# Self-attention probabilities transposed by VectorE in 32x32 squares and rearranged by sixteen SBUF transfers, in place of TensorE transposes

## The reference, cut to what matters

```python
step = s // 4
scale = q[:, ::step].reshape(b, -1)
qk = jnp.einsum('bsd,btd->bst', q, k)
scaled_qk = qk * scale[:, None, :]
softmax_qk = jax.nn.softmax(scaled_qk, axis=-1)
return jnp.einsum('bst,btv->bsv', softmax_qk, v)
...
x = x + _L0_attn_ref(_layernorm(x, axis=-1), L0_attn_k, L0_attn_v, L0_attn_scale_factor, L0_attn_dropout_p)
```

## Time and profile before

| | |
|---|---|
| median of the three runs | 3894.85 us |
| lowest, highest | 3888.32, 3895.75 us |
| span of the profiled execution, first to last instruction | 3891.2 us |
| TensorE busy in that span | 3788.4 us (97%) |
| VectorE, ScalarE, GpSimd busy | 2395.0, 1432.7, 1534.5 us |
| the attention's tile loop | about 28 to 817 us of the span |

### The profile page before, as it was taken

One profiled execution on the slowest core, in us unless ns is written; L12 is line 12 of the kernel. 1 busy time (PEld: TensorE's weight loads), 2 busy tenths in 40 slices (PEclk: granted clock), 3 DMA queues, 4 the chain that ended last, 5 costly groups with the idle time before them and its releaser, 6 DMA issues. The chain is left out here.

```text
span 3891.2 us, 63669 instructions
## 1 busy us (share of the span) xinstructions
PE 3788.4 (97%) x19001; PEld 2532.2 (65%) x19161; DVE 2395.0 (62%) x6222; ACT 1432.7 (37%) x1793; POOL 1534.5 (39%) x860
## 2 busy tenths in 40 slices
PE   8999999999999899999999999999999999999998
PEld 7888888888877444544444444544444777777776
DVE  6544444444458688888888788878887533433135
ACT  3111222233224455455545555445555221222332
POOL 1000000000013667766677666766665222312234
PEclk9999999999999999999999999999999999999999
DMA  4001000145555322222112222222111433328579
GB/s 157 32 32 32 32 32 32 44 172 178 191 179 186 94 57 55 57 57 46 35 38 57 58 57 58 54 57 55 33 36 49 151 126 132 114 92 278 185 263 332
DMA packets 223177, 381.89 MB, mean 98 GB/s; under 512 B 17544, under 2 KB 102056, under 8 KB 222892
## 3 DMA queue, kind: packets, MB, share of 16 engines
q1 hardware_dynamic: 192876, 301.34, 26.7%
q0 software_dynamic: 14752, 49.29, 3.5%
q10 hardware_dynamic: 15264, 27.79, 1.9%
HBM read 229.71 MB, written 148.66 MB: 97 GB/s over the span
## 5 line engine op out<-in xcount | busy, mean ns | idle before, releaser
L1103 DVE CUSTOM_DVE_ANT_0 xf_unread<-xa_mx_ps,mask_q 128x402 bf16<-128x402 f32 x1984 | 1036.0, 573 | 290.3 <-PE xa_mx_ps L1096 156.7
L1726 ACT ACTIVATE probs<-xa_scores 128x1024 f32<-128x1024 f32 (+1 forms) x416 | 417.5, 1024 | 417.0 <-PE xa_scores L1600 371.6
L1726 ACT ACTIVATE xa_probs<-xa_scores 128x1024 f32<-128x1024 f32 (+1 forms) x416 | 417.3, 1024 | 397.8 <-PE xa_scores L1600 355.1
L1561 POOL TENSOR_TENSOR xa_sums<-xa_sums,xa_probs 128x1024 f32<-128x1024 f32 x220 | 519.7, 2383 | 18.1 <-POOL xa_sums L1561 15.7
L1561 POOL TENSOR_TENSOR xa_sums<-xa_sums,probs 128x1024 f32<-128x1024 f32 x220 | 519.3, 2381 | 18.9 <-POOL xa_sums L1561 15.3
L1600 PE MATMUL xa_scores<-mask_t,ident_b 128*128 128x512 bf16 (+1 forms) x1505 | 499.7, 387 | 5.3 <-issue 0.2
L1096 PE MATMUL xa_mx_ps<-xa_kp,queries 96*128 96x402 f32 x1024 | 364.2, 418 | 0.8
L1096 PE MATMUL xa_mx_ps<-xf_kp,queries 96*128 96x402 f32 x960 | 341.5, 418 | 0.4
L1594 PE MATMUL xa_scores<-queries,xf_kp 97*128 97x512 f32 (+1 forms) x832 | 284.2, 423 | 16.3 <-ACTq L1748 8.2
L1096 PEld LDWEIGHTS xa_mx_ps<-xa_kp,queries 96*128 96x128 f32 x1024 | 181.7, 189 | 172.2 <-DVE xf_maxima L1103 111.6
L1594 PE MATMUL xa_scores<-queries,xa_kp 97*128 97x512 f32 (+1 forms) x832 | 284.7, 423 | 1.8 <-ACT probs L1726 1.8
(11 more groups left out here) (415 smaller groups left out, 7388.0 us busy)
## 6 DMA issues: line engine op xcount, KB each, us to landing
bridge_rows<-sorted_in SPq DMA_DIRECT2D x78, 256.0 KB
sorted_out<-ex_made ACTq DMA_DIRECT2D x78, 256.0 KB
queries<-qT_high SPq DMA_DIRECT2D x30, 512.0 KB
xf_kp<-kT_high SPq DMA_DIRECT2D x16, 800.5 KB, 12.4
xa_kp<-kT_high SPq DMA_DIRECT2D x16, 800.5 KB
rows<-in_ctx SPq DMA_DIRECT2D x16, 768.0 KB, 5.1
values<-cxl_v SPq DMA_DIRECT2D x48, 256.0 KB
kT_high<-cxl_kT_high SPq DMA_DIRECT2D x12, 768.0 KB, 4.0
```

The costliest lines, as they stand in the source:

```text
L1103: return dve.tensor_tensor_reduce(out=unread[slot % 2][:, :], in0=scores[:, 0:MKEYS], in1=mask_q[:, half * QB + qt, MFIRST[kb]:MFIRST[kb] ...
L1561: pool.tensor_tensor(sums[pr][:, :, :], left[pr][:, :, :], right[pr][:, :, :], ALU.add).then_inc(pool_added, 1)
L1726: act.activation(prob[ring][pr][0:keys, :, :], scores[pr][0:keys, :, :], ACT.Exp, scale=SCALE).then_inc(exped, 1)
```

## The change

The probabilities no longer go through TensorE and PSUM.

- `turn_p` is now one VectorE instruction for a tile, a transpose of 128 x 2048 elements in squares of 32 x 32, from `prob` to `scaled`. It stands behind `row_max(t + 1)` and `low_n(t + 2)` and waits for `exp(t + 1)`.
- Squares alone are not a full transpose, since a 32-partition strip stays in its own strip. `move` on SP therefore issues 16 transfers of 32 partitions x 512 elements (64 KB each, 1 MB in all) from `scaled` back to `prob`; each brings one strip of queries of one strip of keys to its place. It stands in SP's loop between `load_add(t + 1)` and `store(t + 1)`.
- `high_p` on ScalarE reads the four groups from `prob` in SBUF, once all 16 transfers have landed.
- `low_p` moves to GpSimd, four instructions a tile, behind `step(t + 2)`.
- The scores of a tile are now multiplied into `scaled` only when the transfers of the tile ahead have landed (`wait_moved` in `scale_block`), and `exp` writes `prob` only when `low_p` of the tile ahead is done.
- TensorE's tile is four banks of scores, `turn`, four groups of `weigh`. In the last tile 9 of the 15 groups of `turn_last` come ahead of `weigh`.

```diff
+        prob_by_key = prob.rearrange("p j (c a k) -> p a (j c) k", a=QB, k=SQUARE)
+        squares = scaled.rearrange("p a (c q) -> p a c q", q=SQUARE)
+        raw_pT = prob.rearrange("p i (c q) -> p c i q", q=SQUARE)
...
+                def move(t):
+                    sp.wait_ge(p_turned, t + 1)
+                    for a in range(QB):
+                        for i in range(QB):
+                            sp.dma_start(prob[a * SQUARE:(a + 1) * SQUARE, i, :],
+                                         scaled[i * SQUARE:(i + 1) * SQUARE, a, :]).then_inc(p_in, 16)
...
                 load_add(0)
+                move(0)
                 for b in range(1, B):
                     load_scale(b)
+                move(1)
                 store(0)
                 with sp.Fori(0, tiles - 3) as t:
                     load_norm(t + 3)
                     load_add(t + 1)
+                    move(t + 2)
                     store(t + 1)
...
+                def low_p(t):
+                    for j in range(NB):
+                        mine = slice(j * KB, (j + 1) * KB)
+                        pool.wait_ge(pT_high, NB * t + j + 1)
+                        pool.tensor_tensor(pT[1][:, mine, :].rearrange("p c (i q) -> p c i q", q=SQUARE), raw_pT[:, mine, :, :],
+                                           words(pT[0][:, mine, :]).rearrange("p c (i q) -> p c i q", q=SQUARE),
+                                           ALU.subtract).then_inc(pT_low, 1)
...
-                def turn_p(t, j):
-                    if j == 0:
-                        pe.wait_ge(exped, t + 3)
-                    pe.wait_ge(pT_low, NB * t + j + 2)
-                    for n in range(KB):
-                        last = pe.transpose(pT_ps[j % 2][:, n, :], prob[:, j, n * P:(n + 1) * P], ident[:, :])
-                    last.then_inc(p_turned, 1)
...
                 def exp(t):
-                    act.wait_ge(p_turned, NB * t + 1 + NB)
+                    act.wait_ge(pT_low, NB * (t + 1))
                     act.wait_ge(peak, t + 3)
...
                     if j == 0:
                         act.wait_ge(weighed, t + 2)
-                    act.wait_ge(p_turned, NB * t + j + 2 + NB)
-                    act.activation(pT[0][:, j * KB:(j + 1) * KB, :], pT_ps[j % 2][:, :, :], ACT.Copy).then_inc(pT_high, 1)
+                        wait_moved(act, t)
+                    mine = slice(j * KB, (j + 1) * KB)
+                    act.activation(pT[0][:, mine, :].rearrange("p c (i q) -> p c i q", q=SQUARE), raw_pT[:, mine, :, :],
+                                   ACT.Copy).then_inc(pT_high, 1)
...
                 def scale_block(t, j):
                     if j == 0:
-                        dve.wait_ge(exped, t + 2)
+                        wait_moved(dve, t - 1)
...
+                def turn_p(t):
+                    dve.wait_ge(exped, t + 3)
+                    dve.transpose(squares[:, :, :, :], prob_by_key[:, :, :, :]).then_inc(p_turned, 1)
```

More of the change, by code:

```diff
@@ L30 @@
 BANK = 512
+SQUARE = 32
+QB = P // SQUARE
+MOVED = 16 * QB * QB
 EPS = 1e-5
@@ L130, in self_attention @@
         nT_ps = ps("nT_ps", [P, DC, P])
-        pT_ps = [ps(f"pT_ps{i}", [P, KB, P]) for i in range(2)]
+        k_ps = [ps(f"k_ps{i}", [P, KB, P])[:, :, :] for i in range(2)]
         o_ps = ps("o_ps", [P, D])
-        k_ps = [pT_ps[0][:, :, :], pT_ps[1][:, :, :], o_ps[:, :].rearrange("p (c n) -> p c n", n=P)]
+        k_ps.append(o_ps[:, :].rearrange("p (c n) -> p c n", n=P))
         raw_in = [sem(f"raw_in{i}") for i in range(ARRIVALS)]
@@ L156, in self_attention @@
         p_turned = sem("p_turned")
+        p_in = sem("p_in")
         pT_high, pT_low = sem("pT_high"), sem("pT_low")
@@ L167, in wait_v_split, with wait_moved @@
             eng.wait_ge(v_low, T1C - POOL_V)
+        def wait_moved(eng, t):
+            eng.wait_ge(p_in, MOVED * (t + 2))
         GROUPS_W = len(weights) * DC
         LAST_GROUPS = GROUPS_W + FULL
+        AHEAD = GROUPS_W - FULL
         def last_source(n):
@@ L231, in _ @@
                     load_add(t)
+                    if t == tiles - 2:
+                        move(t + 1)
                     if t == tiles - 1:
-                        sp.wait_ge(exped, tiles + 2)
+                        wait_moved(sp, tiles - 1)
                         sp.dma_start(opening.rows[:, 0, 0:FULL, :],
                                      context[0][0:FULL * P, :].rearrange("(r p) n -> p r n", p=P)).then_inc(rows_in, 16)
-                        sp.wait_ge(p_turned, NB * tiles + NB + 1)
+                        sp.wait_ge(pT_low, NB * tiles + NB)
                         sp.dma_start(opening.rows[:, 1, 0:FULL, :],
@@ L266, in _ @@
                                        ALU.subtract).then_inc(v_low_pool, 1)
[L267 to L272, removed]
+                pool.sem_inc(pT_low, NB)
+                for t in range(B + 1):
+                    step(t + 2)
+                    low_p(t)
+                    if 0 < t < B:
+                        scale_step(t)
+                with pool.Fori(0, tiles - 3 - B) as t:
+                    step(t + B + 3)
+                    low_p(t + B + 1)
+                low_p(tiles - 2)
+                low_p(tiles - 1)
             @block.tensor
@@ L333, in tile @@
                 def tile(t, ahead):
[L334 to L340, removed]
+                    for j in range(NB) if ahead >= 1 else ():
+                        score(t + 1, j)
                     if ahead >= 2:
                         turn(t + 2)
+                    for n in range(AHEAD) if ahead == 0 else ():
+                        turn_last(n)
                     for j in range(NB):
                         weigh(t, j)
[L345 to L349, removed]
+                        if ahead == 0 and AHEAD + j < GROUPS_W:
+                            turn_last(AHEAD + j)
+                    for n in range(GROUPS_W, LAST_GROUPS) if ahead == 0 else ():
                         turn_last(n)
                 pe.sem_inc(turned, 2)
-                pe.sem_inc(p_turned, NB + 1)
                 pe.sem_inc(weighed, 2)
@@ L392, in tile @@
                 def tile(t, ahead):
-                    high_p(t, 0)
-                    high_p(t, 1)
+                    for n in range(NB) if ahead == 0 else ():
+                        high_last(n)
+                    for j in range(NB):
+                        high_p(t, j)
+                        if ahead == 0:
+                            high_last(NB + j)
+                    for n in range(2 * NB, LAST_GROUPS) if ahead == 0 else ():
+                        high_last(n)
                     if ahead >= 2:
                         high_n(t + 2)
[L397 to L402, removed]
                     if ahead >= 1:
@@ L537, in tile @@
                     next_scales(t, NB - 1)
[L538 to L542, removed]
+                    if ahead >= 1:
+                        turn_p(t + 1)
+                    for n in range(AHEAD) if ahead == 0 else ():
                         low_last(n)
                     add(t)
-                    for n in range(NB * FULL - FULL, LAST_GROUPS) if ahead == 0 else ():
+                    for n in range(AHEAD, LAST_GROUPS) if ahead == 0 else ():
                         low_last(n)
@@ L575, in _ @@
                     low_v(i)
+                turn_p(0)
                 for t in range(B + 1):
```

10 lines of the change are left out of this document (2 added, 8 removed).

## The result

| | before | after |
|---|---|---|
| median of the runs beside each other | 3895.3 us (4 runs) | 3979.17 us (4 runs) |
| lowest, highest | 3888.32, 3898.31 us | 3976.28, 3980.65 us |
| ratio, 95% interval | | 1.0222 [1.0207, 1.0236] |
| span of the profiled execution | 3891.2 us | 3978.5 us |
| last sum of the attention (`add(31)`), us from the span's start | 812.57 | 904.14 |

The kernel is 2.2% slower. The forecast said slower, at 3910 us, but its range ended at 3952 us. In the profiled execution 91.6 us are lost in the attention; the later stages, which the change does not touch, took 4 us less.

What follows compares the result with a forecast made beforehand. The prediction took the ring through SP's queue, 24.19 us a tile against TensorE's 22.65, as the new bound. The stage ends 15.4 us later: 3891.2 + 15.4 = 3906.6, with 3.65 for the median 3910 us; range 3860 to 3952.

Steps and rivals of the forecast that it cites:

- sixteen issues: SP's burst of transfers in each tile: 0.475 us from one issue to the next, 7.60 us in all.
- ring: Attention loop from SP's store and load through VectorE and ScalarE to the next transfers: 24.19 us a tile, over TensorE's 22.65.
- The bounds: SP's transfers: one issue costs 0.38 us from below, 0.475 from above; the range's own part used 0.46 to 0.48.
- dear squares: Rival on VectorE's transpose: 3.63 us, kernel 3950, or 5.0 and near 3991; chance 0.14, shared with `low_p` over 1.6 us.
- hand-overs: Three passes from engine to engine in a tile's round, 0.1 us each, 0.30 in all.
- What stood beside the ring: Transfers' landing, `high_p` and four `low_p` cost nothing: `low_p` ends 5.3 us after the power, the maximum 6.3.
- The squares: VectorE's one-instruction transpose of a tile: 2.29 us, taken from the maximum's time; 1.88 from below, 3.63 from above.
- The collision: VectorE's normalising beside GpSimd's `low_p`: 1.37 us to the first scale block, alone 0.47; rival without it 3878 us, chance 0.13.
- The start: First tiles of the attention: `move(2)` ends at 99.6 us, then 29.4, 29.4 and 27.6 more to `move(5)` at 186.0.
- The clock: TensorE's clock may fall to 1.2 GHz at its stops: nothing put in, up to 8 us in the range.

Runs made afterwards that it cites:

- twelve-transfer run: Changed kernel with twelve of the sixteen transfers, the last strip of keys left unmoved; 3895.85 us, ratio 1.0013 to the kernel before.
- early load: Changed kernel with `load_norm` of a tile further ahead issued ahead of `move`; 3854.61 us, ratio 0.9899 to the kernel before.
- two queues: Changed kernel with eight of the sixteen transfers issued from ScalarE's queue and eight from SP's; 3847.59 us, ratio 0.9881 to the kernel before.
- both remedies: Changed kernel with early load and two queues together; 3835.68 us, ratio 0.9858 to the kernel before.

## Why the prediction was wrong

**The step that failed** is the term "sixteen issues: ... I take 0.475, as sixteen stand in a burst: 7.60". They measured 10.02 us and 0.17 more to the store: 0.633 us from one to the next. The rows it was taken from, have no transfer with both ends in SBUF (the first two go from DRAM to 32 partitions of SBUF, the third from 128 partitions of SBUF to DRAM, and not 32, as the rows' heading says), and the argument "0.475 is the spacing in rows 8, whatever is issued" carried it over to transfers from SBUF to SBUF. Reading DRAM in the same place gave 0.464 back. 2.5 us in a ring that is gone round 30 times is 75 us: 828.0 forecast for the last sum and 904.14 measured are 76.1 apart. Nothing else is needed for the miss. The median is only 69 us above the forecast because the later stages took 4.3 us less, and the median lies 0.6 us above the profiled span, where the forecast added 3.65. The twelve-transfer run, which puts the forecast's 7.5 us in place, comes to within 11 us of the forecast's sum.

**The bounds** failed with it. The issue was bounded from 0.36 to 0.475 by the nearest rows, and the upper end was taken as the value, so the range had no room above for them. The range did reach to 3952, but for dear squares.

**The ring** was right: its path, its order and every other term within 0.05 us, the hand-overs excepted (0.1 in place of 0.3). The early load and the two queues each cut it at a different place, and each time TensorE became the bound at 22.56 us. What stood beside the ring was right too: in the changed kernel `low_p` ends at 633.26 and the maximum at 634.36, 1.1 us apart where the forecast has 1.0 (5.3 against 6.3 us after the power; four times its 1.36 would be 5.4).

```profile
628.10 5.16 POOL L287 TENSOR_TENSOR sa_pT_low<-rows,sa_pT_high 128x512 fp32r<-128x512 f32 x4
```

**The squares** took 2.31 us for 2048 elements, as long as the maximum. The rival of dear squares (3.63, or the estimated 5.0 us by the Trainium skill, "VectorE: DVE Perf Modes", section "The three transpose paths", which gives 311 ns for 128x128 in bf16) did not happen; one instruction over float32 took less than half of sixteen times that figure:

```profile
L490 DVE STREAM_TRANSPOSE rows<-rows x32: 2301/2312/2315, 42.1 to 873.6; 128x2048 f32<-128x2048 f32 x32
```

**The collision** of normalising and `low_p` was there, 1.48 us for 0.55; the rival gave 32 us for taking it out (27 of the ring, 5 of tiles 2 to 4), and neither way of doing so was worth more than some 14. With `low_p` held back it started later, and became later than the maximum (626.08 against 625.66). With `low_p` on VectorE all of the collision is gone, in tiles 2 to 4 as well, but the statistics wait for the subtractions. For the factors of the other batches the forecast has two normalisings 0.9 us longer each; in tiles 2 and 3 they took 0.89, 1.54 and 0.53 us beside `low_p`, and 0.54 each without it.

**The start**: `move(2)` was forecast to end at 99.6 and ended at 104.8; with twelve transfers it ended at 98.2. From there to `move(5)` the bursts begin 31.3, 31.6 and 28.9 us apart; less 2.5 for the issues that is 28.8, 29.1 and 26.4, where the forecast has 29.4, 29.4 and 27.6. In tiles 2 and 3 some 0.5 us of the difference is the normalisings of factors, which the forecast had too long.

**The clock** was put at nothing (up to 8 us in the range), and that held, although the clock fell further than forecast (0.94 over the loop). TensorE's stops before `turn` differ from tile to tile. After one of 1.01 us the matmuls start 0.23 us apart, at the level of 2.4 GHz (but for the first, 0.31); after one of 3.90 us they start 0.43 apart for 3.5 us, as at the level of 1.2 GHz, and the granted clock from 628 to 632 us is 0.78:

```profile
603.02 0.66 PE L317 MATMUL sa_nT_ps<-ident,sa_normed 128*128 128x128 f32 x4 [1.01 <-DVE sa_normed L468]
603.44 0.47 PE L47 MATMUL sa_o_ps<-sa_v_high,sa_pT_high 128*128 128x512 f32 x1
603.75 0.39 PE L48 MATMUL sa_o_ps<-sa_v_low,sa_pT_high 128*128 128x512 f32 x1
603.98 0.39 PE L49 MATMUL sa_o_ps<-sa_v_high,sa_pT_low 128*128 128x512 f32 x1
...
629.70 0.65 PE L317 MATMUL sa_nT_ps<-ident,sa_normed 128*128 128x128 f32 x4 [3.90 <-DVE sa_normed L468]
630.11 0.67 PE L47 MATMUL sa_o_ps<-sa_v_high,sa_pT_high 128*128 128x512 f32 x1
630.58 0.63 PE L48 MATMUL sa_o_ps<-sa_v_low,sa_pT_high 128*128 128x512 f32 x1
631.01 0.63 PE L49 MATMUL sa_o_ps<-sa_v_high,sa_pT_low 128*128 128x512 f32 x1
```

The sum moves by that (614.81, then 643.12, which is 28.3 apart), but the bursts on SP stay 26.5 to 26.9 us apart, since the store waits in SP's queue until 622.37 in any case. The slow matmuls fall into time in which TensorE would have waited.

**What stays open.** From the last sum to the end it took 3078.6 us before, 3074.4 after, and 3071.6 and 3070.3 with twelve transfers and with both remedies. Each is one profiled execution, and fifteen runs of the kernel before, in one series, lay from 3885.80 to 3901.32 us, so these 4 to 8 us cannot be told from its spread. That a burst with both ends in SBUF takes 0.633 us an issue, and one that reads DRAM in its place 0.464, is shown; why is not.

## What to carry to other kernels

When a change puts a burst of transfers into a queue, count the issues, not the bytes, and see what stands behind them in that queue: here a load of 256 KB stood 10 us behind sixteen issues on which it does not depend. Take the price of an issue from a row with the same kinds of source and destination, and where there is none, leave the range open upwards, since an error in a ring is multiplied by its rounds. Before giving up such a change, move what is urgent ahead of the burst, or split the burst over two issuing engines: either turned 2.2% slower into about 1% faster (ratios 0.9899 and 0.9881).

## What the runs showed of the hardware

- An issue of a transfer from SBUF to SBUF takes 0.59 us of the issuing queue, one every 0.633 us in a burst; from DRAM to SBUF in the same place 0.42 and 0.464. From SBUF to DRAM, in another stage of the kernel before, one took 0.43 and the next began 0.48 later. From SBUF to SBUF it is nearly the same for 128 partitions (four issues in 2.44 us), and the same for 32 and 64 KB.
- Two queues (SP's and ScalarE's) issue at the same time, SP's with the spacing it has alone (0.633 us) and ScalarE's with 0.643 us; ScalarE's was never run alone.
- VectorE turns 128x2048 float32 in squares of 32x32 in 2.31 us in one instruction.
- A subtraction of 128x512 by GpSimd that runs beside VectorE's normalising of 128x512 float32 from SBUF makes the normalising 1.48 us long instead of 0.55; scale blocks (which read scores in PSUM) beside the same subtractions keep their length, 2.47 us for four (2.48 with the low part on VectorE), and so does the maximum, 2.29 us.
